# Moving the subtraction of the halved counts from VectorE to GpSimd in the comparison loop

## The reference, cut to what matters

```python
vc = v - jnp.mean(v, axis=2, keepdims=True)
v_exp = jnp.concatenate([vc, jnp.zeros_like(vc)], axis=2)
context_s = _eff_if_sorted(v_sorted, Z_sort)      # a * Z - b, with a, b running sums
sum_relu = _eff_if_sorted(vns, Z_sort)            # the same with v = 1
norm_sorted = 2.0 * sum_relu - (Z_sort * total_v - total_vz)
norm = jnp.maximum(norm, 0.0001)
context = 2.0 * context / norm[..., None]
```

## Time and profile before

| | |
|---|---|
| median of 3 runs | 1160.4 us (1157.96 to 1162.7) |
| the profiled execution | 1157.91 us, span 1156.1 us |
| comparison loop | about 132 to 281 us of the span |
| VectorE busy over the span | 739.5 us (64%) |
| GpSimd busy over the span | 519.6 us (45%) |
| ScalarE busy over the span | 658.7 us (57%) |

### The profile page before, as it was taken

The page is one execution under the profiler, slowest core; times in us unless marked ns, Lnnn a source line. Parts: engine busy times, 40 slices in busy tenths (PEclk is TensorE's granted clock), DMA queues, the critical chain, the costliest instruction groups (busy, mean ns, idle before and its releaser), DMA issues. The chain is left out here.

```text
span 1156.1 us, 20054 instructions
## 1 busy us (share of the span) xinstructions
PE 837.6 (72%) x5810; PEld 686.2 (59%) x5812; DVE 739.5 (64%) x2343; ACT 658.7 (57%) x1352; POOL 519.6 (45%) x635
## 2 busy tenths in 40 slices
PE   3796666763439999976995466667567999999900
PEld 2633555653328889976993233444346989999900
DVE  5578699998765547112676699998986451005646
ACT  4354888885734226653664566777665656666500
POOL 0001766663046666667774775000003666025264
PEclk9998788787558999997997768899785999999955
DMA  7970000001501136645763111000004133233232
GB/s 202 290 214 0 1 1 0 0 0 59 200 28 44 44 98 180 192 137 165 197 169 104 46 46 35 1 0 1 1 6 170 44 96 112 72 86 102 58 93 62
DMA packets 133847, 97.03 MB, mean 84 GB/s; under 512 B 11649, under 2 KB 125697, under 8 KB 132737
## 3 DMA queue, kind: packets, MB, share of 16 engines
q1 hardware_dynamic: 121472, 70.79, 20.5%
q0 software_dynamic: 12288, 25.19, 7.5%
HBM read 45.61 MB, written 50.33 MB: 83 GB/s over the span
## 5 line engine op out<-in xcount | busy, mean ns | idle before, releaser
L1178 POOL DMA_INDIRECT e_xs<-h_tok,rows_of x128 | 129.3, 1011 | 103.6 <-issue 69.9
L747 ACT ACTIVATE mask<-ps_q,k_neg 128x256 bf16<-128x256 f32 x256 | 100.9, 488 | 13.1 <-PE ps_q L906 11.9
L1191 POOL DMA_INDIRECT e_got<-e_ys,e_rows_of x64 | 66.0, 1032 | 93.8 <-DMA e_ys<-e_y_rows 67.9
L1819 DVE TENSOR_TENSOR e_hidden<-e_ps_gu,e_hidden 128x512 f32<-128x512 f32 x48 | 33.2, 691 | 95.8 <-ACT e_hidden L1502 95.5
L1327 PE MATMUL e_ps_gu<-e_w_all,e_x_turned 128*128 x384 | 91.7, 382 | 0.5 <-ACT e_x_turned L1496 0.5
L1178 POOL DMA_INDIRECT e_xs<-h_tok,e_rows_of x64 | 65.6, 1025 | 50.2 <-DVEq L1661 17.2
L1359 PE MATMUL e_ps_up<-e_x_turned,e_w_up 128*128 128x128 f32 x640 | 84.5, 275 | 1.0 <-ACT e_x_turned L1496 1.0
L2314 POOL DMA_INDIRECT c_got<-e_ys,rows_of x64 | 71.3, 1113 | 29.7 <-issue 19.2
L1370 PE MATMUL e_ps_y<-e_w_all,e_hidden 128*128 x640 | 84.2, 275 | 0.0
L653 DVE TENSOR_TENSOR mask<-ps_q,k_tok 128x1024 bf16<-128x1024 f32 x64 | 75.1, 1214 | 11.2 <-PE ps_q L894 9.2
L1828 DVE COPY e_y_rows<-e_ps_y 128x512 f32<-128x512 f32 x20 | 13.8, 691 | 105.6 <-PE e_ps_y L1370 105.6
(11 more groups left out here) (400 smaller groups left out, 2419.3 us busy)
## 6 DMA issues: line engine op xcount, KB each, us to landing
e_x_rows<-e_xs SPq DMA_DIRECT2D x68, 256.0 KB, 3.2
e_ys<-e_y_rows SPq DMA_DIRECT2D x68, 256.0 KB, 2.5
e_xs<-zeros SPq DMA_DIRECT2D x2, 6144.0 KB, 34.2
e_w_all<-in_w SPq DMA_DIRECT2D x4, 1536.0 KB, 12.9
e_xs<-zeros SPq DMA_DIRECT2D x2, 2560.0 KB, 27.5
e_w_all<-in_w SPq DMA_DIRECT2D x4, 1024.0 KB, 9.9
x_tok<-in_x SPq DMA_DIRECT2D x4, 512.0 KB, 6.0
e_xs<-h_tok,rows_of POOLq DMA_INDIRECT x128, 2.3
```

Of the source, the lines that this page charges most:

```text
L747: last = nc.scalar.activation(mask[parity][QS // 2 + pair // 2][keys][:, h * T:(h + 1) * T], psq[1][:, h * T:(h + 1) * T], ACT.Sign, bias= ...
L1178: nc.gpsimd.indirect_dma_start(out=xs[part], out_offset=bass.IndirectOffsetOnAxis(ap=rows_of[:, t * K + k:t * K + k + 1], axis=0), in_=til ...
L1191: nc.gpsimd.indirect_dma_start(out=got[t % GB][:, k * P:(k + 1) * P], out_offset=None, in_=ys[part], in_offset=bass.IndirectOffsetOnAxis(a ...
```

## The change

GpSimd gets a third instruction in `numerators`: behind its own subtraction (and a wait for it, on `num_own`, which now counts two for each batch) it subtracts the halved counts from the ninth column into `n1` and raises `num_out`. VectorE's `results` loses that subtraction, so its chain begins with the maximum.

```diff
-                    steps = 3
+                    steps = 2
...
                         dve.wait_ge(num_out, FROM + b_ + 1)
-                        c.link(nc.vector.tensor_tensor(n1[:, :], num3[:, :, HD],
-                                                       at(half_counts, b_ * (TPB * HEADS), TPB * HEADS), ALU.subtract))
                         c.link(nc.vector.tensor_scalar(n1[:, :], n1[:, :], 0.5e-4, None, ALU.max))
...
+                        own = FROM + b_ * 2
                         nc.gpsimd.tensor_tensor(num3, S[:, :, 0:HD + 1], q_b, ALU.mult).then_inc(num_own, 1)
-                        pool.wait_ge(num_own, FROM + b_ + 1)
-                        nc.gpsimd.tensor_tensor(num3, num3, S[:, :, HD + 1:VC], ALU.subtract).then_inc(num_out, 1)
+                        pool.wait_ge(num_own, own + 1)
+                        nc.gpsimd.tensor_tensor(num3, num3, S[:, :, HD + 1:VC], ALU.subtract).then_inc(num_own, 1)
+                        pool.wait_ge(num_own, own + 2)
+                        nc.gpsimd.tensor_tensor(n1[:, :], num3[:, :, HD],
+                                                at(half_counts, b_ * (TPB * HEADS), TPB * HEADS),
+                                                ALU.subtract).then_inc(num_out, 1)
```

## The result

The changed kernel takes 1162.97 us in the median of ten runs (1160.32 to 1165.92), the kernel before 1159.15 us in ten (1155.19 to 1162.7). The ratio is 1.0038 with a 95% interval of 1.0020 to 1.0055: about 4.4 us slower (the medians lie 3.8 us apart), by an amount that is small but clear of zero, and inside the 0.5% that was called "within". The profiled execution after took 1160.32 us, its span is 1158.5 us.

A forecast was written before the change was run, and what follows sets the result against it. VectorE was taken to set the pace, with GpSimd holding its small instructions. Thirteen chains lengthened by 0.25 or 0.35 us, with small corrections, gave +4 us on the 1160.4 us median: 1164.4 us, range 1157 to 1168.

The forecast's parts named there:

- within: Whole run: time changes by no more than about 0.5%, 5.8 us, either way; chance 0.80.
- The price of the new instruction: GpSimd, behind the numerators: subtraction 0.25 us plus 0.15 gap, moving later GpSimd work by 0.40 us, bounds 0.31 and 0.57.
- The maximum lands in the third part: VectorE's maximum, held by GpSimd's L826, which starts 0.07 us ahead: about 0.65 us instead of 0.18, ending 0.04 after it.
- The product lands in the remainder: VectorE's L679, held by GpSimd's L821, ends 0.27 us after it: 0.25 or 0.35 us later than before, by chain.
- the first kind: One of two kinds of VectorE chain in the comparison loop; seven such held chains counted, each 0.25 us longer.
- The sum of a pair: Comparison loop: a pair of batches takes 18.4 us instead of 17.80.
- The sum over the loop: Comparison loop: 7 x 0.25 + 6 x 0.35 = 3.9 us, small corrections, together +4 us, bounds 2.7 and 6.1.
- ScalarE's later middle part at nothing: ScalarE's second part of tile 1, waiting for moved L821, costs nothing: ScalarE has 2.63 us to spare over two batches.
- the maximum first: Rival: VectorE's maximum runs before GpSimd's third part takes hold; about 0.3 us gained per batch, -4 us, 1156.4; chance 0.10.
- Only the maximum is held: Rival: VectorE's product is not held, each batch loses 0.18 us; +2.4 us, 1162.8; chance 0.12.
- Nothing moves: Rival: VectorE's slack elsewhere takes the change up; 0 us, 1160.4; chance 0.08.
- dear: Rival: GpSimd's new subtraction pays for its input's extent, 0.78 us; +11 us, 1171.8; chance 0.08.

## Why the prediction was right

Its range and its sign held, and the mechanism held step by step. In the sum one term was too small and one chain was not counted, and the total came out closer than its parts.

- *The price of the new instruction*: estimated 0.25 us and a gap of 0.15; measured 0.26 and 0.16. Its moved successors follow by 0.4 us, as taken.
- *The maximum lands in the third part*: forecast to take 0.65 us and to end 0.04 us behind it; 0.65 and 0.03. The lead of 0.07 us is there: the third part starts at 186.15, the maximum at 186.22.
- *The product lands in the remainder*: forecast 0.27 us behind its end, measured 0.28. From the end of the reductions to the end of the product it was 186.19 - 182.39 = 3.80 us in the first kind and is 188.00 - 183.94 = 4.06, 0.26 more (forecast 0.25); in the second 3.67 became 4.05, 0.38 more (forecast 0.35).
- *The sum of a pair*: a pair of batches was forecast at 18.4 us and takes 18.52. Of the 0.12 us that were missed, 0.04 are in the products above and 0.08 stand behind the product of the first kind: from its end to the next comparison it was 186.73 - 186.19 = 0.54 us and is 188.62 - 188.00 = 0.62, with the statistics at 0.55. What stretches them I did not look into.
- *The sum over the loop*: over the five pairs from batch 3 to 12 the loop lost 3.68 us (3.0 forecast). Batches 0 to 2, with the first two chains, lost 0.75 (0.60 forecast). From batch 13 on the loop gained 0.12, where the forecast has a loss of 0.25. The sum has a miscount there: seven, six, one and the last are 15 chains, but there are 16, and 14 of them have a third part and a remainder behind the numerators and are held, not 13. Batches 13 and 14 lost 0.27 and 0.30 us. The stretch from batch 15 on gained 0.69, because the 15th chain, which I had counted at 0, is shorter and VectorE no longer waits 0.43 us for TensorE behind it. Together 4.31 against 4.0: the misses have both signs, so that the total fits this well is in part luck. The time on record, 1164.4 us, stands on a median of three runs, 1160.4; ten runs of the kernel before have 1159.15, which is most of the distance to the 1162.97 measured.
- *ScalarE's later middle part at nothing*: borne out by the run with the third part first, in which the remainder that this part waits for comes 0.8 us sooner after the second pair of comparisons begins (187.21 - 184.93 = 2.28 us against 186.98 - 183.86 = 3.12) and a pair of batches gains 0.04 us.
- *The rivals*: "the maximum first" did not happen, the third part's start leads. "Only the maximum is held" falls with a product of 0.60 us (its 2.4 us alone the interval would just have let stand), and the run with the reciprocal first shows that it is the product's hold that sets the end. "Nothing moves" and "dear" fall with the interval and with 0.26 us.
- *The rule of the Trainium skill* (SBUF — State Buffer, Who interferes with whom, The single rule), that the first of the two to issue keeps the other out for its whole length, agrees with these traces where one starts 0.03 us or more ahead of the other. They add that a held product ends 0.28 us behind the GpSimd instruction, and not its own 0.42; at 0.01 us the recorded starts do not tell who is held (see the end). The Trainium skill's statement, in the same section, that an instruction with one SBUF input outside the two-port modes does not contend agrees with the reciprocal, which has 0.34 to 0.35 us in all of these profiles, under any GpSimd instruction; whether the reciprocal has a two-port mode that section does not say.

## What to carry to other kernels

Where VectorE and GpSimd work side by side as here, price a small VectorE instruction by the GpSimd instruction it will fall into, not by its own length: lay the two timelines over each other and ask which one starts first. Taking work off VectorE can lengthen its chain if the work goes into the GpSimd run that holds it, and an instruction taken out ahead of a hold buys little; what counts is where the last held instruction comes to lie. A chain that begins with an instruction which is not held, here the reciprocal, can cross a GpSimd instruction for free: with that, and without a floor for a difference below zero, the same move made the fastest kernel of this study, 1151.83 us. How much of a shorter chain the kernel keeps depends on what VectorE waits for next: there it was 0.54 us for each pair of batches.

## What was not expected of the hardware

- A lead of 0.01 us does not always decide. At the start of the loop, in the changed kernel, GpSimd's columns start 0.01 us ahead of VectorE's tensor_scalar, and it is GpSimd that is held (0.58 us instead of 0.29), while in the earlier trace rows a lead of 0.05 us and above a lead of 0.03 us decided for GpSimd. In the run with the third part first, in the 14th chain, a lead of 0.01 us did decide for GpSimd: its third part starts at 271.82, the product at 271.83, and the product is held to 0.28 us behind it. The rows of the first case:

```profile
138.32 0.58 POOL L805 COPY cols<-v_tok 128x128 f32<-128x128 f32 x1
138.33 0.41 DVE L642 TENSOR_SCALAR half_counts<-q_tok 128x512 f32<-128x512 f32 x1
```

- The 256-column product ends 0.27 to 0.29 us after the GpSimd instruction that holds it, whether that is the third part, the remainder or the columns' multiplication, and the 32-column instructions end 0.03 to 0.06 us after it. It is so in every held chain of the comparison loop in these profiles, so with the starts known the ends of the held instructions follow to within a few hundredths of a microsecond.
